# TensorE's program in the attention edge stages of a graph network, as loops over batches and pairs of units

## The reference, cut to what matters

```python
xl = x @ W
a_src = (xl * att_s).sum(-1); a_dst = (xl * att_d).sum(-1)
a_edge = ((ea2 @ We) * att_e).sum(-1)
alpha = leaky_relu(a_src[src2] + a_dst[dst2] + a_edge, 0.2)
amax = segment_max(alpha, dst2)
ex = exp(alpha - amax[dst2])
den = segment_sum(ex, dst2)
out = segment_sum(xl[src2] * (ex / den[dst2])[..., None], dst2) + bias
```

## Time and profile before

| | us |
|---|---|
| median of 3 runs | 11032.46 |
| lowest, highest | 11007.47, 11046.3 |
| span of the profiled execution | 10914.7 |

### The profile page before, as it was taken

How to read it: one execution, slowest core, us unless ns; L and a number is a source line. 1 busy time by engine, 2 the same in 40 slices (tenths; PEclk the granted TensorE clock), 3 DMA queues, 4 the chain that set the end, 5 groups by cost and what they waited for, 6 DMA issues and landing times. The chain is left out here.

```text
span 10914.7 us, 110752 instructions
## 1 busy us (share of the span) xinstructions
PE 6056.6 (55%) x30283; PEld 4663.6 (43%) x30284; DVE 3780.1 (35%) x5844; ACT 1828.9 (17%) x2603; POOL 6768.8 (62%) x6802
## 2 busy tenths in 40 slices
PE   2677777777677777777413444444470444444446
PEld 1555555555555555555303333333350333333334
DVE  6333333333333333333402223323250232233326
ACT  1333333333333333333200000000010000000000
POOL 2666666666566666666366666666606666666660
PEclk6777777777777777777555555555555555555555
DMA  4222222222222222222321212222112222122211
GB/s 137 64 67 65 67 65 67 65 67 63 76 65 67 65 65 67 65 67 65 72 49 42 46 42 45 46 42 46 37 23 45 48 46 42 42 45 45 44 40 25
DMA packets 376718, 611.95 MB, mean 56 GB/s; under 512 B 173478, under 2 KB 211098, under 8 KB 374875
## 3 DMA queue, kind: packets, MB, share of 16 engines
q0 software_dynamic: 214032, 332.71, 14.4%
q1 hardware_dynamic: 157212, 262.18, 7.6%
q10 hardware_dynamic: 5193, 13.44, 0.4%
HBM read 575.04 MB, written 32.78 MB: 56 GB/s over the span
## 5 line engine op out<-in xcount | busy, mean ns | idle before, releaser
L1171 POOL DMA_INDIRECT big<-xl_table,idx_stage x3328 | 3339.6, 1003 | 1561.5 <-issue 1002.4
L711 POOL DMA_INDIRECT big<-q_table,idx_stage x3328 | 3319.1, 997 | 1580.6 <-issue 949.7
L1442 PE MATMUL bank<-msg,onehot 128*128 128x66 f32 x6656 | 1592.9, 413 | 854.6 <-issue 817.4
L1442 PEld LDWEIGHTS bank<-msg,onehot 128*128 128x128 f32 x6656 | 1501.8, 325 | 1047.4 <-issue 1046.2
L806 PEld LDWEIGHTS bank<-big,wide 128*128 128x128 f32 x6656 | 1212.5, 258 | 1435.1 <-issue 1434.0
L806 PE MATMUL bank<-big,wide 128*128 x6656 | 1258.4, 346 | 772.9 <-DVE wide L742 500.5
L820 PE MATMUL bank<-msg,onehot 128*128 128x67 f32 (+1 forms) x6656 | 1148.9, 322 | 360.6 <-issue 223.8
L802 PE MATMUL bank<-big,ident 128*128 128x512 f32 x1664 | 1242.8, 835 | 140.1 <-DMA big<-q_table,idx_stage 77.8
L820 PEld LDWEIGHTS bank<-msg,onehot 128*128 128x128 f32 x6656 | 1063.2, 238 | 500.5 <-issue 499.6
L1292 DVE TENSOR_TENSOR wide<-wide,bank 128x528 f32 x416 | 292.9, 704 | 2386.7 <-remote 920.6
L1390 PE MATMUL bank<-spread_bf,big 128*128 x3328 | 269.5, 172 | 1386.5 <-issue 1171.9
(11 more groups left out here) (226 smaller groups left out, 3519.8 us busy)
## 6 DMA issues: line engine op xcount, KB each, us to landing
wide<-rel_rows SPq DMA_DIRECT2D x208, 512.0 KB
big<-rel_rows SPq DMA_DIRECT2D x208, 512.0 KB
big<-q_table,idx_stage POOLq DMA_INDIRECT x3328
big<-xl_table,idx_stage POOLq DMA_INDIRECT x3328
q_table<-wide SPq DMA_DIRECT2D x12, 1024.0 KB, 5.1
edge_rows<-big SPq DMA_DIRECT2D x25, 257.0 KB, 7.5
xl_table<-big SPq DMA_DIRECT2D x12, 520.0 KB, 6.7
big<-in_edge_attr ACTq DMA_DIRECT2D x6, 1024.0 KB
```

The source lines that it names most:

```text
L711: pool.indirect_dma_start(out=ring[:, group % UNROLL, s % GROUP, :], out_offset=None, in_=k.q_table, in_offset=bass.IndirectOffsetOnAxis(a ...
L1171: pool.indirect_dma_start(out=buf[p][:, s, :], out_offset=None, in_=k.xl_table, in_offset=bass.IndirectOffsetOnAxis(ap=k.idx_stage[:, s:s ...
L1442: nc.tensor.matmul(sums_of[j][:, ds(slots[i], C + 2)], onehot[j][:, i, :], msg[j][:, i, 0:C + 2], start=False, stop=False)
```

## The change

On TensorE alone, the attention edge stage is written as loops whose counter is the pair of units: one for batch -1, one for batch 0 (its first pair written ahead of it), two nested loops over batches 1 to 10 and their pairs, one for batch 11, and one for batch 12. Batch 11 and what closes it stay apart since its scan pieces come later. The scan pieces stand in every such loop body and run under `pe.If(it == turn)`. The lag of one unit is gone from the way it is written: a pair now issues its own two units. The programs of the other engines are the same.

```diff
--- before.py
+++ after.py
@@ -1423,48 +1423,63 @@
                     last = nc.tensor.transpose(k.psum[4][:, j * P:(j + 1) * P], wx[:, j, :], k.ident[:, :])
                 last.then_inc(s_wt, 1)
 
-            def batch(b, p, turn):
-                first_unit = b * BUNITS
-
-                def sums(it, first, last):
-                    n = counts(pe, first_unit + it * GAT_UNROLL, -1, 1)
-                    step = (b * BIT + it) * ITER
-
-                    def segment_sum(c):
-                        j = c % SETS
-                        slots = load_offsets(k, pe, SPAN_ROW, step + c * UNIT, UNIT, (UNIT - 1) * P)
-                        wait(pe, e_acc, n[c])
-                        open_span(nc, k, sum_pair[j])
-                        wait(pe, e_m, n[c + 1])
-                        wait(pe, e_w, n[c + 1])
-                        wait(pe, e_S, n[c + 1])
-                        for i in range(UNIT):
-                            nc.tensor.matmul(sums_of[j][:, ds(slots[i], C + 2)], onehot[j][:, i, :],
-                                                        msg[j][:, i, 0:C + 2], start=False, stop=False)
-                        close_span(nc, k, sum_pair[j]).then_inc(e_agg, 1)
-
-                    for u in range(GAT_UNROLL):
-                        if not begins(b):
-                            stages(u, first, last, (1, segment_sum))
-                        if spreads(b):
-                            stages(u, first, last, (1, lambda c: expand((b + 2) * BIT + it, (b * BIT + it) * ITER + 2 * P, it * ITER * SLOT, c)))
-                        if not ends(b):
-                            if (it, u) == ((6, 0) if late(b) else (2, 1)):
-                                scores_t(b + 1)
-                            if (it, u) == ((7, 0) if late(b) else (4, 0)):
-                                ends_t(b + 1)
-                            if (it, u) == ((BIT, 1) if late(b) else (5, 0)):
-                                carries_t(b + 1)
-                            if (it, u) == ((BIT, 1) if late(b) else (6, 0)):
-                                factor_all(b + 1)
-                            if (it, u) == ((BIT, 1) if late(b) else (7, 1)):
-                                weights_t(b + 1)
-
-                if spreads(b):
-                    pe.wait_ge(s_near, b + 2)
-                for it in range(BIT + 1):
-                    sums(it, it == 0, it == BIT)
-            over_batches(pe, batch)
+            def segment_sum(b, it, c):
+                n = counts(pe, b * BUNITS + it * GAT_UNROLL, -1, 2)
+                slots = load_offsets(k, pe, SPAN_ROW, (b * BIT + it) * ITER + c * UNIT, UNIT, (UNIT - 1) * P)
+                wait(pe, e_acc, n[c])
+                open_span(nc, k, sum_pair[c])
+                wait(pe, e_m, n[c + 1])
+                wait(pe, e_w, n[c + 1])
+                wait(pe, e_S, n[c + 1])
+                for i in range(UNIT):
+                    nc.tensor.matmul(sums_of[c][:, ds(slots[i], C + 2)], onehot[c][:, i, :],
+                                                msg[c][:, i, 0:C + 2], start=False, stop=False)
+                close_span(nc, k, sum_pair[c]).then_inc(e_agg, 1)
+
+            def at_iteration(it, turn, piece, b):
+                if isinstance(it, int):
+                    if it == turn:
+                        piece(b)
+                    return
+                with pe.If(it == turn):
+                    piece(b)
+
+            def pair(b, it, sums=True, spread=True, scan=True):
+                column = it * (ITER * SLOT)
+                for c in range(GAT_UNROLL):
+                    if sums:
+                        segment_sum(b, it, c)
+                    if spread:
+                        expand((b + 2) * BIT + it, (b * BIT + it) * ITER + 2 * P, column, c)
+                    if scan and c == 0:
+                        at_iteration(it, 2, scores_t, b + 1)
+                        at_iteration(it, 7, weights_t, b + 1)
+                if scan:
+                    at_iteration(it, 3, ends_t, b + 1)
+                    at_iteration(it, 4, carries_t, b + 1)
+                    at_iteration(it, 5, factor_all, b + 1)
+
+            pe.wait_ge(s_near, 1)
+            with pe.Fori(0, BIT) as it:
+                pair(-1, it, sums=False)
+            pe.wait_ge(s_near, 2)
+            pair(0, 0)
+            with pe.Fori(1, BIT) as it:
+                pair(0, it)
+            with pe.Fori(1, NBATCH - 2) as b:
+                pe.wait_ge(s_near, b + 2)
+                pe.sem_inc(s_turn, 1)
+                with pe.Fori(0, BIT) as it:
+                    pair(b, it)
+            with pe.Fori(0, BIT) as it:
+                pair(NBATCH - 2, it, spread=False, scan=False)
+                at_iteration(it, 5, scores_t, NBATCH - 1)
+                at_iteration(it, 6, ends_t, NBATCH - 1)
+            carries_t(NBATCH - 1)
+            factor_all(NBATCH - 1)
+            weights_t(NBATCH - 1)
+            with pe.Fori(0, BIT) as it:
+                pair(NBATCH - 1, it, spread=False, scan=False)
 
 
 def gat_finish(k, layer, out):
```

## The result

The changed kernel takes 11054.75 us (median of 20 runs, 11025.22 to 11070.87), the kernel before, run on the same chips, 11032.27 us (20 runs, 11002.96 to 11046.6). The ratio is 1.0019 with a 95% interval of [1.0012, 1.0025]: slower by some 21 us, which is clear of the noise and still within the 0.3% that the prediction had called no change. 10380 us was forecast. It is the outcome of the second rival, the one that had 0.04.

The account below looks back on a forecast made before the run. POOL and TensorE were taken to bound the attention edge stages in turn, TensorE slowed by code fetches. Gains of 571 + 90 - 6 = 655 us from 11032.5 us gave 10380 us, range 10,310 to 10,620, chance 0.82.

Parts of the forecast that it names:

- second rival: TensorE's slow stretches have nothing to do with code, perhaps gathers of 260-byte rows alone; about 11,030 us, chance 0.04.
- term A: POOL's waits for VectorE's message in both attention edge stages go; 571 us gained of 624 us of waits.
- term B: End of each attention stage: batch 12's scores follow POOL's last gather sooner; 45 us per stage, 90 us gained.
- I read this as code blocks whose fetch is slow while gathers run: TensorE's slow stretches, about 125 of a batch's 191 us, come from code fetches; the shorter loop body removes them.
- rival 1: Some slow stretches stay, as nested loops or skipped pieces still cause fetches; 10,650 us, chance 0.09.
- The rule that was weighed: Straight code is streamed ahead, cost mostly hidden, and taken branches break this; A would then be about 0.
- Term C: TensorE's loop branches, 0.215 us each, hidden under POOL's pace except in the tail; a cost of 6 us.
- far-branch rival: Every taken branch on TensorE is a far one at 3.49 us, 150 us more per batch; 12,230 us, chance 0.05.
- The range's lower end: 10,310 us: all waits and both tails gone, 10,322, with the 25 us spread of earlier runs.

Follow-up runs that it names:

- run 6: Changed kernel; POOL waits, ahead of every unit but the first of a half, until its own attention-stage gathers have landed: 11030.05 us (kernel before 11048.95).
- run 9: Changed kernel; POOL does a tiny memset and waits for it after every fourth gather of the attention edge stages: 10812.75 us, 0.990 of the kernel before.
- run 4: Changed kernel; SP loads the relative targets only for the first pairs, later expansions read old targets: 11025.48 us (kernel before 10994.54).
- run 11: Kernel before (unrolled); POOL waits ahead of every second unit, 16 gathers, until its gathers have landed: 10678.56 us, 0.9787 of the kernel before.
- run 1: Changed kernel; POOL leaves out every odd step's gather in the attention edge stages: 8724.92 us (kernel before 10994.54).
- run 5: Kernel before (unrolled); POOL leaves out every odd step's gather in the attention edge stages: 8770.11 us, 0.7938 of the kernel before.
- run 10: Changed kernel; POOL waits ahead of every second unit, 16 gathers, until its gathers have landed: 10698.73 us, 0.9799 of the kernel before.
- run 14: Changed kernel; 15 more never-true conditions on TensorE in every pair of units that has scan pieces: 10990.48 us, 1.008 of the kernel before.
- run 3: Changed kernel; gathered rows of 256 bytes in place of 260, source term read from the last channel: 11011.63 us (kernel before 10994.54).
- run 8: Changed kernel; each attention-stage gather replaced by a plain DMA of the table's first 128 rows, same bytes and queue: 8096.96 us.
- run 12: Changed kernel; POOL does a tiny memset and waits for it after every eighth gather: 10760.97 us, 0.9881 of the kernel before.
- run 2: Changed kernel; each attention-stage gather replaced by a 128x512 fp32 add on POOL, no rows gathered: 10611.77 us (kernel before 10994.54).

## Why the prediction was wrong

- **The view of the stage was right.** POOL and TensorE hold each other up, and TensorE's speed in its slow stretches sets POOL's waits. Runs 6 and 9 take the slow stretches away, and all waits for messages go, those of the first two batches too, of which I had let half stay because of SP's loads; without those loads, in run 4, the first waits are as long (30.9 us against 30.3 in the changed kernel), so they had no part. So the consequences in term A (no waits) and term B (the scores 3.0 us after the last gather instead of 56, 53 us per stage, the upper end) were worked out correctly from a premise that this change does not bring about. The size of A was not measured, since the pauses of those runs have a price of their own.
- **The step that failed is "I read this as code blocks whose fetch is slow while gathers run".** Terms A (571 us) and B (90 us) hung on it, and both measured nothing: POOL's waits came to 699 us in the two stages against 624, and batch 12's scores to 56.5 us after the last gather against 55.8. What the runs show in its place is that the slow stretches come with indirect gathers at full pace, in a body of 108 rows as in one of 1,337. The step rested on three things. The instruction blocks were there, but were a companion: one is left of 53 and the slow time is as large; and run 11, unrolled, fetches 56 of them in the window of the earlier trace rows with a slow time of 23 and 31. Its row:

```profile
q8 instruction: 56, 0.92, 0.2%
```

  The fast batches 11 and 12 have no gathers, which spoke for the rival as well. And "POOL gathers at the same pace" in CGConv was true of means that count the waits (1.49 us per step against 1.50) and false where it matters: between waits, the attention stages gather for tens of us at 1.25 us, while in CGConv no 16 gathers in a row between 1000 and 2400 us take less than 1.29 each. Its POOL timeline of before has single gathers stretched to 1.46 and 1.76 us (none of its 126 gathers longer than 1.05 us from 1000 to 2400 us is without an operation of VectorE beside it) and a wait every 16:

```profile
1506.22 0.95 POOL L711 DMA_INDIRECT big<-q_table,idx_stage  x1 [0.30 <-issue]
1507.98 1.46 POOL L711 DMA_INDIRECT big<-q_table,idx_stage  x1 [0.81 <-issue]
...
1519.99 1.76 POOL L711 DMA_INDIRECT big<-q_table,idx_stage  x1 [0.30 <-issue]
...
1524.78 0.94 POOL L711 DMA_INDIRECT big<-q_table,idx_stage  x1 [1.78 <-remote]
```

- **A sign in the trace of before was read the other way.** The first expansions of a stage stand in a small loop there (L1394, 8 turns). POOL gathers from 5406.63 us, and TensorE goes slow in that loop as well:

```profile
5444.14 0.17 PE L1390 MATMUL bank<-spread_bf,big 128*128 x1 [0.48 <-issue]
5446.24 0.17 PE L1390 MATMUL bank<-spread_bf,big 128*128 x1 [1.94 <-issue]
```

  The prediction gave this to rival 1, stretches that stay in loops. It speaks at least as much for rival 2, stretches that have nothing to do with code.
- **The rule that was weighed was right on this kernel.** The Trainium skill, "Runtime: NRT & Kernel Launch", section "Instruction fetch mechanics", has straight code streamed with its cost mostly hidden. I noted that the trace disagreed; it was my reading of it that did. In runs 1 and 5 both forms stand at 0.794 of before, and in runs 10 and 11 the unrolled one is at 0.9787 against 0.9799. The page's second half is about taken branches whose target has to be fetched first: the back edge of 3.49 us agrees with it. The short conditions of run 14, at 0.20 us, are another case.
- **Term C** was forecast at 6 us, with branches at 0.215 us hidden under POOL's 169 us. The median is 0.20 us as taken, but the cover was not there, since TensorE stayed on the path. They may be the home of the 21 us: this is by the proportion of 9% above, not by a run that takes them out. Against it, run 1 has 206 us more of them than run 5 and is no slower. So where the 21 us come from stays open. The far-branch rival is out: no branch of L1444 takes more than 0.72 us.
- **The range's lower end** took 25 us off 10,322, which gives 10,297 and not 10,310; nothing hangs on it.
- **What would have decided it beforehand.** To set the starts and ends of TensorE's slow stretches beside POOL's timeline, not only beside the code. A chance of 0.04 for a rival against which there were two arguments, one of them a mean, was too small. Its condition, gathers of 260-byte rows alone, was right about the gathers and, by run 3, not about the size of the rows.

**Open**: by what path indirect gathers slow TensorE, and what exactly the slowing counts. The runs rule out code form, the size of the rows, SP's loads, POOL's own work, the packets into SBUF as such and a backlog. What is left is what sets run 8 apart, the indirect form or its random rows of DRAM, and no run separates the two. Also open is why 32 gathers in a row order the runs and 16 do not: by 16, CGConv has 44 of slow time at a fastest 1.29 us and run 12 has 120 at 1.34.

## What to carry to other kernels

When an engine's instructions come at an even, much longer spacing with nothing waited for, set the edges of such stretches beside every other engine's timeline before blaming its code; a companion that appears in the same stage (here, instruction blocks) is not a cause until its own times match. Where POOL gathers with indirect DMAs and is at times ahead of its consumers, a wait for its own gathers every 16 is worth trying: here 2.3 us per wait bought 2% of the kernel, while the same wait every 8 bought nothing. And compare paces between waits, not means that contain them.

## What was not expected of the hardware

- Indirect gathers of 128 rows, back to back at 1.25 us, bring TensorE's instructions (weight loads, matmuls, register operations, and in run 14 branches) to 0.70 us each, mostly after 12 to 24 us; breaks of 2 us every 10 us take this to almost nothing (run 6), every 20 us to a quarter or less (runs 10 and 11).
- A plain DMA of the same shape costs POOL 542 ns, an indirect one 1,001 ns, and the plain ones did not slow TensorE at over twice the rate (run 8; all of them read the same rows).
- With POOL computing in place of gathering, VectorE's busy time for the same instructions went from 689 us (run 6, 1,290 instructions) to 1,129 us (run 2). The row of run 6:

```profile
5484.00:8049.00 2565.00, 961.34 (x5604) 812.08 (x5604) 689.46 (x1290) 57.61 (x239) 1662.91 (x1690) 0.50 0.20 43
```
